# A two-layer kernel whose pair differences, their absolute value and their exponential are done in four tiles instead of in one piece

## The reference, cut to what matters

```python
g = A[None, None, :] * dt
Lam = jax.nn.softplus(Lp[None, None] * dl)
cg = jnp.cumsum(g, axis=1)
diff = cg[:, :, None, :] - cg[:, None, :, :]
decay = jnp.exp(jnp.where(tri[None, :, :, None], diff, NEG))
...
Wmat = scores * jnp.transpose(decay, (0, 3, 1, 2)) * jnp.transpose(lam_ts, (0, 2, 1, 3))
Y = jnp.einsum('bhts,bshd->bhtd', Wmat, V)
```

## Time and profile before

| | |
|---|---|
| median of 3 runs | 1239.69 us (1239.32 to 1242.14) |
| the profiled execution's own time | 1243.28 us |
| its span, first to last instruction | 1241.1 us |
| mean granted clock of TensorE | 0.955 of full speed |
| busy: PE, DVE, ACT, POOL | 88%, 81%, 56%, 25% of the span |
| length of a pass, passes 3 to 13 | 71.96 to 71.99 us; 5 and 9: 73.66 and 73.68; 6 and 10: 72.48 and 72.49 |

### The profile page before, as it was taken

How to read it: one execution, slowest core, us unless ns; L and a number is a source line. 1 busy time by engine, 2 the same in 40 slices (tenths; PEclk the granted TensorE clock), 3 DMA queues, 4 the chain that set the end, 5 groups by cost and what they waited for, 6 DMA issues and landing times.

```text
span 1241.1 us, 17991 instructions
## 1 busy us (share of the span) xinstructions
PE 1094.8 (88%) x5756; PEld 672.9 (54%) x5756; DVE 1002.7 (81%) x2141; ACT 698.2 (56%) x1366; POOL 310.4 (25%) x197
## 2 busy tenths in 40 slices
PE   5799989998998989999898999999898998989882
PEld 3455636555564655556465555646555564655641
DVE  4688796978979697896979789697978969797667
ACT  4382845738375573837557383655828375573661
POOL 0040220504114050411405041140504114050283
PEclk9799989899999999899999999989999999999885
DMA  3000000000000000000000000000000000002126
GB/s 130 9 9 4 6 17 9 17 8 0 17 8 17 8 17 8 0 17 8 17 8 17 8 0 17 8 17 8 17 8 0 17 8 17 8 17 69 50 94 203
DMA packets 32562, 28.64 MB, mean 23 GB/s; under 512 B 1568, under 2 KB 26144, under 8 KB 32288
## 3 DMA queue, kind: packets, MB, share of 16 engines
q1 hardware_dynamic: 32544, 28.42, 6.9%
HBM read 16.09 MB, written 12.32 MB: 23 GB/s over the span
## 4 chain that ended last, share of the span: by engine, by line
PE 53%; DVE 34%; issue 9%; ACT 2%; DMA 1%; DVEq 0%; SPq 0%; POOLq 0%; POOL 0%; ACTq 0%
DVE ms L1248 6%; PE p L462 5%; PE p L581 4%; PE p L619 3%; DVE skip L1080 3%; PE p L544 3%; PE p L477 3%; PE p L479 2%; PE p L478 2%; PE p L556 2%; PE p L570 2%; DVE pair L1321 2%; PE p L433 2%; DVE nodesT L1257 2%; PE p L424 2%
## 5 line engine op out<-in xcount | busy, mean ns | idle before, releaser
L1509 POOL TENSOR_TENSOR pair<-pair,cgt 128x2048 f32<-128x2048 f32 x16 | 58.4, 3648 | 799.8 <-DVE pair L1308 799.8
L852 ACT ACTIVATE gx<-p 128x512 f32<-128x512 f32 x256 | 143.6, 592 | 14.9 <-PE p L479 9.3
L477 PE MATMUL p<-x1Th,Gl 128*128 128x512 f32 x256 | 120.0, 469 | 4.0 <-ACT gx L852 4.0
L812 ACT ACTIVATE gelu<-p,bias_u 128x512 f32<-128x512 f32 x32 | 22.0, 687 | 153.6 <-PE p L424 153.6
L479 PE MATMUL p<-x1Th,Gh 128*128 128x512 f32 x256 | 101.9, 398 | 0.0
L478 PE MATMUL p<-x1Tl,Gh 128*128 128x512 f32 x256 | 101.6, 397 | 0.0
L1522 POOL TENSOR_TENSOR vp<-vdw,beta 128x384 f32<-128x384 f32 (+3 forms) x80 | 80.8, 1043 | 56.0 <-DVE beta L1300 56.0
L544 PE MATMUL p<-gx,x1T 128*32 128x512 f32 x512 | 74.1, 653 | 15.2 <-DVE pair L1325 14.4
L581 PEld LDWEIGHTS p<-vbd,pair 128*128 128x128 f32 x512 | 62.8, 193 | 43.0 <-issue 34.4
L1248 DVE TENSOR_TENSOR ms<-lam,K 128x64 f32<-128x64 f32 (+4 forms) x80 | 84.5, 1132 | 0.0
L394 PE MATMUL p<-xnT,MC 128*128 128x512 f32 x64 | 38.0, 680 | 46.5 <-DVE y L1153 46.5
(11 more groups left out here) (239 smaller groups left out, 2707.1 us busy)
## 6 DMA issues: line engine op xcount, KB each, us to landing
xin<-in_x SPq DMA_DIRECT2D x16, 256.0 KB, 2.8
hx_scratch<-vdw SPq DMA_DIRECT2D x16, 256.0 KB, 2.5
res_scratch<-res SPq DMA_DIRECT2D x15, 256.0 KB, 2.0
W<-in_weights SPq DMA_DIRECT2D x1, 1477.5 KB, 9.0
gx<-hx_scratch SPq DMA_DIRECT2D x5, 256.0 KB, 3.9
out<-gx SPq DMA_DIRECT2D x5, 256.0 KB, 2.7
gx<-in_weights SPq DMA_DIRECT2D x1, 1216.0 KB, 11.4
GT<-hx_scratch SPq DMA_DIRECT2D x4, 256.0 KB, 4.0
```

The source lines that it names most:

```text
L477: pe.matmul(head_bank(h)[:, :], tile(Gl, h), x1Th[:, :], start=True, stop=False)
L852: act.activation(tile(gx, h, T), head_bank(h)[:, :], ACT.Copy).then_inc(R["gx_copied"], 1)
```

## The change

The subtraction on GpSimd, the absolute value and the exponential on ScalarE are each cut into four instructions of 512 columns. Each of the four counts up its semaphore, and what follows waits for the count of its own tile: each absolute value for its difference, each exponential for its absolute value, and each first product of `pair_weights` for its exponential (before, only the one of tile 0 waited, for all). The line numbers of the changed kernel are up to 2 higher.

```diff
             def pair_decay(i):
 
-                act.wait_ge(R["diff_ready"], i + 1)
-                act.activation(pair[:, :], pair[:, :], ACT.Abs).then_inc(R["diff_abs"], 1)
-                act.wait_ge(R["diff_abs"], i + 1)
-                act.activation(pair[:, :], pair[:, :], ACT.Exp, scale=-1.0).then_inc(R["decay_ready"], 1)
+                for n in range(TILES):
+                    act.wait_ge(R["diff_ready"], 4 * i + n + 1)
+                    act.activation(tile(pair, n, 512), tile(pair, n, 512), ACT.Abs).then_inc(R["diff_abs"], 1)
+                for n in range(TILES):
+                    act.wait_ge(R["diff_abs"], 4 * i + n + 1)
+                    act.activation(tile(pair, n, 512), tile(pair, n, 512), ACT.Exp, scale=-1.0).then_inc(R["decay_ready"], 1)
...
                 if later(i):
-                    dve.wait_ge(R["diff_ready"], i)
+                    dve.wait_ge(R["diff_ready"], 4 * i)
...
             def pair_weights(i, n):
-                if n == 0:
-                    dve.wait_ge(R["decay_ready"], i + 1)
+                dve.wait_ge(R["decay_ready"], 4 * i + n + 1)
                 dve.wait_ge(R["lam_ps"], 4 * i + n + 1)
...
                 pool.wait_ge(R["cgrow_ready"], i + 1)
-                pw = view(pair[:, :], "p (m t) -> p m t", t=CHUNK)
-                pool.tensor_tensor(pw, pw, spread(cgt[:, :].unsqueeze(2), [128, 64, CHUNK]), ALU.subtract)\
-                    .then_inc(R["diff_ready"], 1)
+                for n in range(TILES):
+                    pw = view(tile(pair, n, 512), "p (m t) -> p m t", t=CHUNK)
+                    pool.tensor_tensor(pw, pw, spread(cgt[:, H * n:H * n + H].unsqueeze(2), [128, H, CHUNK]), ALU.subtract)\
+                        .then_inc(R["diff_ready"], 1)
```

## The result

The changed kernel takes 1223.41 us (median of four runs, 1223.13 to 1228.2) against 1240.91 for the kernel before on the same chip: ratio 0.987, interval 0.984 to 0.990. Timed again on another chip it took 1223.69 against 1243.27, ratio 0.985 (0.983 to 0.988).

What follows compares the result with a forecast made beforehand. The chain of waits lay 53% on PE and 34% on DVE, with L1278 stalled behind GpSimd's subtraction. Terms -5.3 + 0.5 - 2.2 = -7.0 us; against the median 1239.7 this gives 1232.7, said as 1232, range 1225 to 1241.

Steps and rivals of the forecast that it cites:

- The mechanism: GpSimd's subtraction and VectorE's L1278, L1235, L1285 take turns at piece ends, L1144 running meanwhile; 0.38 us gained per pass.
- Rival (1): At GpSimd's four pieces: it keeps its place for all, L1278 ends 0.6 us later than now; 1248.5 us, chance 0.07.
- Rival (2): GpSimd's subtraction pieces take 1.27 us each, as L1542; +0.30 us per pass, 1244.4 us in all; chance 0.06.
- rival (3): Piece near 1.19 us, ScalarE's 0.55 reaching the path, or clock taking back 2 us or more; 1236 to 1243, chance 0.19.
- price of a piece: GpSimd's subtraction of 512 columns: 1.10 us, from 1.66 ns per column and 0.25 us per instruction.
- I count the 14 passes, 14 x 0.38 = 5.3: Gain of 0.38 us in each of the loop's 14 passes, 5.3 us; nothing for pass 0 or pass 15.
- The clock term, -2.2: TensorE's stretches at 1.2 GHz in passes 5, 6, 9, 10 cost 4.3 us; half expected gone, -2.2 us.
- The +0.5 of pass 15: ScalarE's eight pieces delay what follows in pass 15, where no idle time covers it: +0.5 us once.

Runs made afterwards that it cites:

- the four kernels with the collision: Kernel before (1240.91 us); only GpSimd cut (1230.74); uncut, L1144 ahead of L1278 (1226.49); changed kernel without added waits (1228.19): VectorE's L1248 run against GpSimd's products in pass 1.
- the second profile: The changed kernel as it is, nothing altered, timed and profiled once more on another chip: 1223.69 us, ratio 0.985.

## Why the prediction was wrong in size

**The mechanism was right.** L1278 ends 0.28 behind the second piece; L1235 takes 1.67 (1.7 predicted); the fourth piece ends 4.84 behind the first's start (4.9); the activations take 4.25 (4.3); the added waits cost nothing in passes 2 to 13, though 0.2 us in pass 0 (69.23 and 69.21 with them, 69.03 without); and every pass at full clock gains the same 0.55. Rival (1), no turns, is out by each of 16 L1280. The Trainium skill, page "SBUF — State Buffer", section "Who interferes with whom", is right that the second one blocks for the whole of the running instruction; the trace adds that an operation of VectorE that is waiting gets in between two GpSimd instructions issued back to back. Rival (2), pieces of 1.27, is out too, and so is rival (3), nothing measurable, by the interval.

**The step "price of a piece" was mis-sized.** I had 1.10 us, from 1.66 ns per column and 0.25 per instruction; it is 1.05. The four sizes now measured lie on a line: 0.61 (256 columns), 1.05 (512), 1.92 (1024), 3.65 (2048), that is 1.70 ns per column and 0.18 per instruction. The 0.25 came from a product of another shape (L1522). Not all of it reaches the path. Piece two ends 0.10 earlier than I had it (2.05 against 2.15), piece four 0.07 (4.84 against 4.91), since from a turn to the end of the next piece I had 0.90 and it is 0.91. The other 0.07 at the first L1285, which ends at 4.92 instead of 5.06, was not the piece: it ends 0.08 behind piece four, where I had 0.15. That makes 0.52 of gain at this point against 0.38. A whole pass gains 0.55; the last 0.03 is not explained.

**The step "I count the 14 passes, 14 x 0.38 = 5.3" was too small and one pass short.** It is 14 x 0.55 = 7.7, and 0.34 to 0.36 in pass 0, where I had counted nothing, on the ground that VectorE soon waits for TensorE there. Without the added waits pass 0 gains 0.54 (69.57 to 69.03), like any other. Together 8.0.

**A term was missing: pass 1.** I read the passes from 3 on, and the three added waits only as a cost. They are worth 4.0 us on the kernel before (1240.46 to 1236.43). Taken out of the changed kernel they cost 0.3 to 0.5% (ratio 0.990 against 0.987 and 0.985), some 4 to 6 us, less surely known since those were timed on different chips. In the profiles 3.35 of it is pass 1 itself (77.00 to 73.65).

**The clock term, -2.2, was too small.** In passes 5 to 10, from which it was worked out, it came near: they held 4.4 us above six full passes, then 1.65. What it left out is the other passes. From the profile of before to the first after: passes 2 to 13 hold 4.90 us above twelve full passes, then 3.33; pass 14 shrinks by 2.22, of which 0.55 is the pass; pass 1 shrinks by 1.68 more than the collision and its 0.55. That is 1.57 + 1.67 + 1.68 = 4.9 us (6.6 with the second profile). Together 8.0 + 3.35 + 4.9 = 16.3, by which the distance from pass 0 to pass 15 shrank (1092.76 to 1076.45). The 4.9 are what is left when the rest is taken off; that it is the clock rests on the granted clock, which is below 1.00 in every pass that is so lengthened. The beginning and the end of that pair of profiles, 3.5 more, lie within the spread of all fourteen. I could not have computed the clock term; I could have said that passes 1, 2 and 14 have such stretches too (0.93, 0.95, 0.96). The direction did not hang on it: 8.0 of the 17.5 us come from the mechanism that was forecast.

**The +0.5 of pass 15** is not shown. In the second profile the first L914 starts 19.68 behind that pass's first piece, against 19.13 before, but in the first profile at 19.12, and it can't be told from the spread of the end.

**What stays open.** What fills the 0.16 us before the third L1075. In the four kernels with the collision it starts 0.31 us behind the second in the first pass of the loop, against 0.07 in pass 3; a later instruction (L1335) is 0.24 late too in that pass, but there the profile names a wait for TensorE. With the three waits neither is seen. A stall of the instruction fetch would fit, and the Trainium skill, page "Runtime: NRT & Kernel Launch", section "Instruction fetch mechanics", says that instructions are fetched in blocks and that a taken branch can cause a fetch stall. No run here shows the fetch itself. Also not explained: why GpSimd's first piece starts 0.09 us later against VectorE with two and eight pieces than with one and four, and what sets the granted clock in the beginning, and the length of the end.

## What to carry to other kernels

When two engines exclude each other, draw the turns instruction by instruction: cutting the long one only hands the stall on, and pays by what the other engine can do without the shared operands meanwhile. So look first for such an operation to move under the long instruction; here that, with the three waits, gave the same as all cuts. Read every pass of a loop, the first and the last above all: an engine that arrives 0.06 us late at a shared resource lost 3.4 us, and three waits elsewhere decided it.

## What the runs showed of the hardware

- GpSimd's fp32 subtraction costs 0.18 us + 1.70 ns per column, from 256 to 2048 columns; back to back, a piece starts 0.04 us before the one in front ends.
- An operation of VectorE with both operands in SBUF that arrives during a piece ends 0.28 us (256 columns) or 0.68 (640) behind it, and delays the next piece by the same order (1.23 and 1.63 instead of 1.05). One with an operand in PSUM took 0.68 beside a piece and 0.69 beside the uncut instruction, as long as alone.
- Three waits that are met long before they are reached changed the time by 4 us: with them the third L1075 of pass 1 is not late. Why is not shown.
- What a stretch of TensorE at 1.2 GHz costs depends on where it falls. Before and in the changed kernel it is 1.65 to 1.70 us for one that begins 58 to 60 us into a pass (before: passes 5 and 9), 0.5 for the long one 13 us into it (passes 6 and 10), and nothing for a short one there (pass 5 of the changed kernel, clock 0.98, 71.43 us). With `own_level` moved, two passes with such a short one (5 and 11) were 1.1 us longer all the same. A pass that got 0.83 us shorter was lengthened in 9 of 13 cases instead of one or two.
